# Score tiles read ahead of the unit's products on VectorE, in a fused attention and expert kernel

## What is computed

```python
pooled = cond(x, W1, b1, v, prompt_type)        # masked softmax pooling in a sequence
scores = einsum('bqhd,bkhd->bhqk', q, k)        # 16 heads of 8
scores = scores + einsum('bqr,bkr->bqk', q_rope, k_rope)[:, None]   # rope term, one for all heads
scores = where(causal, -inf, scores / scale)
w = softmax(scores, axis=-1)
x = x + einsum('bhqk,bkhd->bqhd', w, v) @ W_o
h = einsum('bsd,bdh->bsh', x, W[cat_ids]) + b[cat_ids]
# 64 experts, 8 of them weighted for a token (cw); every expert is computed for every token
y = sum over e of cw[e] * ((silu(h @ Wg[e]) * (h @ Wu[e])) @ Wd[e])  + shared expert
x = x + y
```

## Time and profile before

| | |
|---|---|
| median of 3 runs | 723.68 us (723.67 to 724.1) |
| the profiled execution, its own time | 725.9 us |
| its span, first to last instruction | 724.0 us |
| mean granted clock of TensorE in it | 0.992 of full speed |
| instructions | 15734 |
| busy: TensorE, VectorE, ScalarE, GpSimd | 697.4, 544.5, 442.7, 425.6 us |

### The profile page before, as it was taken

One profiled execution on the slowest core, in us unless ns is written; L12 is line 12 of the kernel. 1 busy time (PEld: TensorE's weight loads), 2 busy tenths in 40 slices (PEclk: granted clock), 3 DMA queues, 4 the chain that ended last, 5 costly groups with the idle time before them and its releaser, 6 DMA issues.

```text
span 724.0 us, 15734 instructions
## 1 busy us (share of the span) xinstructions
PE 697.4 (96%) x5606; PEld 544.1 (75%) x5606; DVE 544.5 (75%) x1146; ACT 442.7 (61%) x857; POOL 425.6 (59%) x351
## 2 busy tenths in 40 slices
PE   7878899899999999999999999999999999999997
PEld 5656677677887778777787778877787777887885
DVE  5777669686697787887688865976878876886664
ACT  3865865477555865478455675558654685565554
POOL 3626696865555655566455654566455664666665
PEclk9989999999999999999999999999999999999999
DMA  8272554345344445435544464444465344355441
GB/s 269 75 285 81 154 131 117 89 123 154 104 130 111 139 106 130 138 101 155 116 110 131 117 149 109 127 114 143 107 126 144 92 146 123 108 127 146 129 131 45
DMA packets 65117, 92.93 MB, mean 128 GB/s; under 512 B 7696, under 2 KB 26576, under 8 KB 65040
## 3 DMA queue, kind: packets, MB, share of 16 engines
q1 hardware_dynamic: 61008, 87.06, 44.5%
q10 hardware_dynamic: 4032, 4.87, 1.9%
HBM read 88.37 MB, written 3.15 MB: 126 GB/s over the span
## 4 chain that ended last, share of the span: by engine, by line
PE 70%; ACT 8%; DVE 8%; SPq 6%; issue 4%; DMA 2%; POOL 1%; POOLq 0%; DVEq 0%
PE banks L1026 68%; DVE hid L984 2%; SPq L316 2%; SPq L310 2%; ACT banks L543 2%; ACT s_t L424 2%; DVE hid L1002 2%; PE banks L1108 1%; ACT L543 1%; DVE k_blk L710 1%; ACT hid_hi L555 1%; ACT L424 1%; DMA gbias<-in_gate_bias 1%; DVE pt_sb L685 1%; POOL hid_lo L657 1%
## 5 line engine op out<-in xcount | busy, mean ns | idle before, releaser
L657 POOL TENSOR_TENSOR hid_lo<-hid,hid_hi 128x512 fp32r<-128x512 f32 (+1 forms) x264 | 343.3, 1300 | 255.8 <-ACT hid_hi L555 253.9
L984 DVE TENSOR_TENSOR hid<-banks,cwb 128x512 f32<-128x512 f32 x252 | 173.2, 687 | 117.1 <-ACT banks L543 114.4
L543 ACT ACTIVATE banks<-banks 128x512 f32<-128x512 f32 x252 | 146.1, 582 | 129.6 <-PE banks L1026 127.9
L555 ACT CAST hid_hi<-hid 128x512 fp32r<-128x512 f32 (+1 forms) x264 | 162.6, 616 | 79.3 <-DVE hid L1002 78.6
L1002 DVE TENSOR_TENSOR hid<-hid,banks 128x512 f32<-128x512 f32 (+1 forms) x262 | 180.0, 687 | 27.9 <-PE banks L1026 5.8
L1026 PE MATMUL banks<-c_hi,wg_hi 128*128 128x512 f32 x264 | 119.0, 451 | 5.6 <-POOL wu_lo L622 2.3
L1026 PE MATMUL banks<-hid_hi,wd_hi 128*128 128x512 f32 (+1 forms) x264 | 104.6, 396 | 0.8 <-POOL hid_lo L657 0.8
L1026 PE MATMUL banks<-c_hi,wu_hi 128*128 128x512 f32 x256 | 102.0, 398 | 2.3 <-DVE hid L1002 2.3
L1026 PE MATMUL banks<-c_hi,wg_lo 128*128 128x512 f32 x264 | 103.5, 392 | 0.0
L1026 PE MATMUL banks<-c_lo,wg_hi 128*128 128x512 f32 x264 | 103.5, 392 | 0.0
L1026 PE MATMUL banks<-hid_lo,wd_hi 128*128 128x512 f32 (+1 forms) x264 | 103.4, 392 | 0.0
(11 more groups left out here) (160 smaller groups left out, 799.6 us busy)
## 6 DMA issues: line engine op xcount, KB each, us to landing
cwb<-cw_scratch SPq DMA_DIRECT2D x254, 256.0 KB, 3.8
k_blk<-in_cond_w SPq DMA_DIRECT2D x112, 64.0 KB
xf<-in_x_feat SPq DMA_DIRECT2D x8, 256.0 KB, 4.0
out_feat<-y ACTq DMA_DIRECT2D x8, 256.0 KB, 3.6
wg_raw<-in_we_gate SPq DMA_DIRECT2D x3, 512.0 KB, 7.5
wu_raw<-in_we_up SPq DMA_DIRECT2D x3, 512.0 KB, 8.0
wd_raw<-in_we_down SPq DMA_DIRECT2D x3, 512.0 KB, 9.4
xf<-in_x_tok SPq DMA_DIRECT2D x6, 256.0 KB, 2.8
```

The costliest lines, as they stand in the source:

```text
L543: nc.scalar.activation(dst, gate_bank(p)[:, :], ACT.Silu).then_inc(S["silu_done"], 1)
L555: nc.scalar.copy(hid_hi[0:n, slot(b, p), :], hid[0:n, slot(b, p), :]).then_inc(S["hi_ready"], 1)
L657: nc.gpsimd.tensor_sub(hid_lo[0:n, slot(b, p), :], hid[0:n, slot(b, p), :], hid_hi[0:n, slot(b, p), :].bitcast(F32)).then_inc(S["lo_ready" ...
L984: nc.vector.tensor_mul(hid[:, slot(b, p), :], gate_bank(p)[:, :], cwb[:, p % NCW, :])\
```

## The change

In VectorE's program, in blocks with b > 0, the steps 6 to 9 of the following block's attention (the add and the maximum of one score tile) are issued at the start of their unit, ahead of the wait for SiLU and the two products, instead of behind the products. In unit 3 they come after the previous block's sum. The list `now` holds the unit's steps; `following` is b + 1, and the last block has no such steps. So six blocks' units change, four units in each. Block 0 and all other engines stay as they are.

```diff
@@ -975,6 +975,9 @@
                 if p == NH - 1 and prev:
                     total(b - 1)
                 first = b == 0 and p < 4
+                scores = [step for step, blk in now if 6 <= step < 10] if prev else []
+                for step in scores:
+                    attention_step(step, following)
                 dve.wait_ge(S["silu_done"], b * UNITS + p + 1)
                 if p < NPAIR and not first:
                     loaded = b * NPAIR // NCW + p // NCW + 1 - (1 if p % NCW < 2 else 0)
@@ -1008,7 +1011,8 @@
                 for step, blk in now:
                     if step == 0:
                         rotate(blk)
-                    attention_step(step, blk)
+                    if step not in scores:
+                        attention_step(step, blk)
                     if step == LOW:
                         rest_of_input(blk, 1 - par)
```

## The result

The changed kernel takes 737.41 us (median of 4 runs, 736.01 to 738.19) against 723.67 (723.0 to 724.1): 1.0185 times the kernel before, 95% interval 1.0165 to 1.0206, or 13.7 us more. The forecast was 738.2. The profiled execution took 738.02, its span 736.1.

A forecast was written before the change was run, and what follows sets the result against it. TensorE, busy 96%, was taken to bound the kernel, with VectorE's delay reaching it through ScalarE's cast and exponentials. Six blocks of 2.42 us give 14.5, so 723.7 + 14.5 = 738.2 us; range 732 to 746.

The forecast's parts named there:

- The wait in unit 1: VectorE idles ahead of tile 0's add until TensorE's score products release it; lost cover delays unit 4's second product 1.33 us.
- The cast of unit 4: On ScalarE it waits for VectorE's hidden tile and starts 2.42 us later; table load and exponentials follow equally late.
- the wait at the first transposes: TensorE stands some 1.9 us for the late exponentials; with the later copy, 2.42 us per block.
- the gate waits: TensorE waits at units 3 and 5's gate products for VectorE's first products, 0.1 to 0.3 us each; counted at nothing.
- lost cover: Without TensorE's 1.9 us wait at the transposes to hide them, the waits at gate products cost 0.4 us per block.
- The rival of the falling clock: TensorE's clock falls after the new wait, 1.7 us per block: 748.4 if in all six, 741.6 in two; chance 0.13.
- The delay was not absorbed: Rival: exponentials on ScalarE do not stand behind the cast, leaving only gate waits, 2.4 us: 726.1; chance 0.07.
- The maxima came no earlier: Rival 'not slower': earlier maxima bring exponentials forward, removing TensorE's 0.24 us wait per block: 722.2; chance 0.04.
- the hold-up passed on in full: Block 0's waiting cast on ScalarE delays TensorE's transposes fully; the reason for taking 2.42 us per block.
- the chain leave TensorE at one place per block: The chain ending last steps onto ScalarE at unit 5's gate product, six times, returning to TensorE some 8 us later.

The follow-up runs named there:

- e4: Kernel before, with only unit 4's add and maximum ahead of their products: 729.6 us against 724.21, ratio 1.0082.
- e6: Changed kernel, with ScalarE's casts of units 4 and 5 behind the third and fourth exponentials and GpSimd's tile 3 subtraction earlier: 729.23 us against 722.51 before.
- e7: e6, plus ScalarE copying the first transposed tile ahead of unit 7's SiLU: 727.39 us against 722.51 for the kernel before.
- e2: Kernel before, with only unit 2's add and maximum ahead of their products: 724.72 us against 724.21, ratio 1.0006.
- e9: Kernel before, with unit 5's cast later and first transposed tile's copy earlier on ScalarE, unit 31's key mask behind unit 32's product on VectorE: 718.77 us against 724.46.
- e1: Kernel before, with only unit 1's add and maximum ahead of their products: 730.3 us against 724.21, ratio 1.0077.
- e5: Kernel before, with only units 1 and 4's adds and maxima ahead of their products: 740.14 us against 722.51, ratio 1.0229.

## Why the prediction was right, point by point

**The wait in unit 1.** VectorE was to idle for about 3 us ahead of the first add; it idled 3.11. All later instructions of the group stand where the sum put them: unit 4's second product at 417.30 (422.28 less 4.98) against 417.33.

**ScalarE.** The cast of unit 4 was to start at 418.05 and stands at 418.02; the wait ahead of it, put at about 1.5, was 1.61, the table load 2.40 later against 2.42. e4 and e6 show that this link carries the cost: the first lengthens it alone, the second cuts it at the cast of unit 4.

**TensorE.** The wait at the first transposes was put at 1.9; the row reads 1.75. It is counted from the end of the last matmul (425.56 + 0.39); in a stream the transposes would have started 0.23 behind that matmul's start, at 425.79, so 1.91 were lost. TensorE got to this point 0.43 later than before (425.79 less 4.98 against 420.38), about 0.2 each from the gate products of units 3 and 5, and 0.43 + 1.91 are the 2.34 by which the first transposes are late. So the 0.4 for the gate waits was right, and that they cost nothing under the longer wait's cover is borne out too: the block is 2.37 longer with them, the table load 2.40 later.

What is left when the cover goes is more than this 0.4: 0.73 in e6. The two gate products cost about 0.2 each there too, and TensorE is 0.47 late ahead of the second transposes. But ScalarE is late as well, for the cast of unit 3, which stands ahead of unit 5's SiLU and the table load, waits for VectorE (ScalarE of e6, b = 4):

```profile
415.30 0.62 ACT L557 CAST hid_hi<-hid 128x512 fp32r<-128x512 f32 x1 [0.95 <-DVE hid L1011]
```

With that the copy comes 0.69 later than before the change (counted from the first score add), and TensorE's wait for it grows from 0.24 to 0.46, which makes 0.69. So e6 cuts the link at one cast and leaves it at another. The prediction's statement for lost cover, and e7's expectation after it, had the gate waits alone and left this cast out.

**The clock.** It stayed at 1.00 around the new wait in each of the six blocks, and the mean over the span was 0.998 against 0.992. The rival of the falling clock did not come.

**The other rivals.** The delay was not absorbed, as ScalarE keeps its order: the table load needs no data from VectorE and still stood behind the waiting cast. The maxima came no earlier in a way that counted, as the row of the first add says, which TensorE's score products release in both kernels. In e2, where a tile goes ahead without a wait or a cost, nothing was gained either.

**The size.** Six blocks with 2.37 are 14.2 us; the medians differ by 13.7, with an interval of 11.9 to 14.9 (0.0165 and 0.0206 of 723.67). The forecast of 14.5 lies in it.

**What the prediction misread.** Two of its readings do not hold, and neither changes the sum. It says that block 0's rows show the hold-up passed on in full; they show 2.92 us at ScalarE's cast and 1.72 at TensorE. What does carry over is the distance from that cast to the transposes: 4.69 in block 0 (70.43 to 75.12), 4.70 after the change (423.00 to 427.70). And it has the chain leave TensorE at one place per block. There is a second, at the end of the blocks of b = 1 to 5, where the chain is on VectorE for some 10 us ahead of the next block's first up product (before, the end of b = 3):

```profile
389.94 0.59 ACT banks L543
...
400.00 0.70 DVE hid L1002
400.75 14.37 PE banks L1026 x210
```

The change does not touch it. The wait there is the one that e9 takes away.

## What to carry to other kernels

Here an instruction that waits for another engine was better put behind the ready work of its own engine: put ahead, it turned that work into a delay, which went from VectorE to ScalarE and on to TensorE. A pair that waited for nothing cost as much (e4), because it stood ahead of what another engine needed. Before moving such a pair, find the consumer with the least slack (here 0.22 us on ScalarE, one cast ahead of the exponentials), and price the move at how much later that one gets its data, not at the wait that appears. Effects of single moves did not simply add up: slack went off once, and one wait hid another.

## What the runs showed that was not expected

The opening stretch, the same code up to unit 0 of b = 1 in before, after and e1 to e5, took 145.61 to 148.93 us in their profiled executions, while the block times of one kernel mostly agree within 0.1 (the third of the five is in most some 0.3 longer). One part of it is TensorE's clock. A wait of 2.36 us for VectorE's first residual sum (L750) stands in both executions, before the change and after it:

```profile
38.14 1.08 PE L1026 MATMUL banks<-wd_raw,x_next 128*32 128x128 f32 x32 [2.36 <-DVE x_next L750]
```

```profile
37.95 1.08 PE L1030 MATMUL banks<-wd_raw,x_next 128*32 128x128 f32 x32 [2.36 <-DVE x_next L750]
```

The granted clock over 36 to 42 was 0.77 before the change (first row) and 1.00 after it (second):

```profile
36.00:42.00 6.00, 3.86 (x38) 2.12 (x38) 2.66 (x4) 2.04 (x4) 2.23 (x2) 0.77 0.98 356
```

```profile
36.00:42.00 6.00, 3.27 (x44) 2.31 (x45) 4.09 (x7) 2.46 (x5) 2.04 (x2) 1.00 0.99 352
```

So after an equal wait at an equal place the clock fell in one execution and not in the other. Where code repeats, the time of one block tells tenths of a microsecond that the medians of the runs cannot.
